# SiLU as one ScalarE function, the second part of the decay exponents as one full-array matmul, and a new order of all queues in a decoder layer

## The reference

```
xn = rmsnorm(x);  proj = xn @ w_in.T          # value, gate, B and C of 16 heads, dt
val = silu(causal_conv4(val) + conv_b)
ld = -softplus(dt + dt_bias) * exp(A_log);  cum = cumsum(ld)
M  = (C @ B.T) * where(tril, exp(cum_l - cum_m), 0)
Y  = M @ v + D_skip * v
out = (Y * silu(gate)) @ w_out.T ; out += 0.5 * memory_read(out) @ w_read.T
x  = layernorm(2 x + out)
x  = layernorm(x + layernorm(attention(x, ctx, mask)))
h  = silu(conv3(quant(x) @ quant(w1).T) + b)  # 512 hidden channels
x  = layernorm(x + quant(h) @ quant(w2).T)
```

## Time and profile before

| what | value |
|---|---|
| median of 3 runs | 895.32 us (894.7 to 895.62) |
| profiled execution, time | 894.32 us |
| profiled execution, span | 892.2 us |
| busy PE / DVE / ACT / POOL | 803.7 / 779.4 / 695.7 / 194.9 us |
| share of the span | 90% / 87% / 78% / 22% |
| granted TensorE clock, mean | 0.953 |
| ended-last chain by engine | PE 51%, DVE 26%, ACT 10%, issue 6% |

### The profile page before, as it was taken

The page is one execution under the profiler, slowest core; times in us unless marked ns, Lnnn a source line. Parts: engine busy times, 40 slices in busy tenths (PEclk is TensorE's granted clock), DMA queues, the critical chain, the costliest instruction groups (busy, mean ns, idle before and its releaser), DMA issues.

```text
span 892.2 us, 21288 instructions
## 1 busy us (share of the span) xinstructions
PE 803.7 (90%) x7928; PEld 589.3 (66%) x7928; DVE 779.4 (87%) x2286; ACT 695.7 (78%) x1372; POOL 194.9 (22%) x237
## 2 busy tenths in 40 slices
PE   3899999999999999999999999999999999966431
PEld 3667677777777677777777776777777777634221
DVE  4565679999999999999999999999999999897755
ACT  2786788888889898898888898988888888754432
POOL 6300013121220313131212202131313121223121
PEclk9899999999999999999999999999999999998555
DMA  6311110211020211110210202011111101000000
GB/s 188 74 18 25 25 37 14 49 33 17 26 48 26 46 28 37 38 37 14 57 16 30 44 25 47 27 38 36 37 25 47 17 28 34 21 18 12 0 12 24
DMA packets 51586, 30.64 MB, mean 34 GB/s; under 512 B 40442, under 2 KB 42444, under 8 KB 51484
## 3 DMA queue, kind: packets, MB, share of 16 engines
q1 hardware_dynamic: 51052, 28.17, 13.8%
q10 hardware_dynamic: 432, 1.11, 0.4%
HBM read 16.68 MB, written 4.19 MB: 23 GB/s over the span
## 4 chain that ended last, share of the span: by engine, by line
PE 51%; DVE 26%; ACT 10%; issue 6%; SPq 2%; POOL 1%; DMA 1%; ACTq 0%; POOLq 0%; DVEq 0%
PE pM L2384 6%; PE pP L2334 5%; PE pP L2336 4%; PE pP L2335 4%; DVE fa L1778 3%; DVE hm L1795 3%; PE pDec L2371 3%; DVE fa L1780 2%; PE pDec L2368 2%; DVE u L1786 2%; ACT L771 2%; DVE ML L1658 2%; DVE conv L1604 2%; PE pC L2507 2%; PE pC L2478 2%
## 5 line engine op out<-in xcount | busy, mean ns | idle before, releaser
L2334 PE MATMUL pP<-xn_hi,G_hi 128*128 128x256 f32 x512 | 157.9, 308 | 1.0 <-ACT P L746 1.0
L746 ACT ACTIVATE P<-pP 128x512 f32<-128x512 f32 x256 | 148.1, 598 | 11.6 <-PE pP L2336 10.5
L2335 PE MATMUL pP<-xn_lo,G_hi 128*128 128x256 f32 x512 | 144.0, 281 | 0.0
L2336 PE MATMUL pP<-xn_hi,G_lo 128*128 128x256 f32 x512 | 143.8, 281 | 0.0
L2384 PE MATMUL pM<-P,xnT 128*64 128x512 f32 x512 | 133.7, 597 | 0.3
L2334 PEld LDWEIGHTS pP<-xn_hi,G_hi 128*128 128x128 f32 x512 | 97.3, 190 | 18.0 <-issue 10.3
L2335 PEld LDWEIGHTS pP<-xn_lo,G_hi 128*128 128x128 f32 x512 | 97.7, 191 | 3.2 <-issue 0.7
L1658 DVE TENSOR_TENSOR ML<-pM,Lm 128x512 f32<-128x512 f32 x128 | 87.6, 684 | 14.0 <-PE pM L2384 11.6
L2336 PEld LDWEIGHTS pP<-xn_hi,G_lo 128*128 128x128 f32 x512 | 97.2, 190 | 0.0
L604 POOL TENSOR_TENSOR rs_c<-ve_c,half_pow 128x4 f32<-128x4 f32 x48 | 48.5, 1011 | 197.8 <-DVE nm_c L1750 100.9
L595 POOL TENSOR_TENSOR u<-u,fa 128x512 f32<-128x512 f32 x32 | 40.8, 1276 | 226.3 <-ACT u L846 226.3
(11 more groups left out here) (240 smaller groups left out, 2055.2 us busy)
## 6 DMA issues: line engine op xcount, KB each, us to landing
v_nat<-vT SPq DMA_DIRECT2D x256, 32.0 KB, 2.1
x_in<-in_x SPq DMA_DIRECT2D x16, 256.0 KB, 2.8
x_res<-in_x SPq DMA_DIRECT2D x16, 256.0 KB, 2.6
ctxT<-in_ctx_t SPq DMA_DIRECT2D x16, 256.0 KB, 3.0
out_x<-x SPq DMA_DIRECT2D x16, 256.0 KB, 2.0
P<-in_wc ACTq DMA_DIRECT2D x2, 512.0 KB, 6.6
P<-in_wb SPq DMA_DIRECT2D x2, 512.0 KB, 9.0
fa<-in_w_t SPq DMA_DIRECT2D x1, 256.0 KB
```

The costliest lines, as they stand in the source:

```text
L746: act.activation(P[:, half, 2 * pair:2 * pair + 2, 0:w], pP[k % 2][:, 0:2 * w].rearrange("p (h l) -> p h l", h=2), ACT.Copy).then_inc(p_co ...
L2334: pe.matmul(dst, w_hi, x_hi, start=True, stop=False)
L2335: pe.matmul(dst, w_hi, x_lo, start=False, stop=False)
L2336: return pe.matmul(dst, w_lo, x_hi, start=False, stop=True)
```

## The change

1. SiLU is one ACT instruction (`ACT.Silu`) for values, gates and all four feed-forward blocks. The products on DVE (values, gates, c = 2, 3) and on POOL (c = 0, 1) go, with their semaphores; so do the factors of 2, and the two set-up instructions for them. The gate part is now freed for pA by ACT itself.
2. conv gets two slots, fa four. `hidden_abs` writes into fa, and the buffer ha goes. The normalised input is written in place (xs is x_in), so the next load of x waits for PE's transposes.
3. A second copy of cum, cum2, holds two column blocks per unit, one for each head of a pair. POOL writes it (`spread_cum`, two instructions per group) from cum3 after `place_cum`, and `decay` of a group's first unit waits for it. The second part of the exponents is then one matmul with 128 array columns.
4. All queues (fill, body, drain) have a new order.

```
-            def value_silu(n, jj):
-                dve.wait_ge(val_tanh.sem, val_tanh.at(n, jj + 1))
-                v = vT[n % 2][:, jj, 0:width(n)]
-                dve.scalar_tensor_tensor(v, v, 1.0, flat(conv[:, 0:seqs_in(n), :]),
-                                         ALU.add, ALU.mult).then_inc(vT_ready.sem, 1)
...
-            def value_tanh(n, jj):
+            def value_silu(n, jj):
                 act.wait_ge(a_read.sem, a_read.at(n, A_VAL[jj]))
                 act.wait_ge(v_nat_ready.sem, v_nat_ready.at(n - 2, 16 * V_MOVES))
                 act.wait_ge(yd_ready.sem, yd_ready.at(n - 2, 2))
-                act.activation(vT[n % 2][:, jj, 0:width(n)], flat(conv[:, 0:seqs_in(n), :]), ACT.Tanh, scale=0.5)\
-                   .then_inc(val_tanh.sem, 1)
+                act.activation(vT[n % 2][:, jj, 0:width(n)], flat(conv[:, jj, 0:seqs_in(n), :]), ACT.Silu)\
+                   .then_inc(vT_ready.sem, 1)
...
-            def gate_tanh_step(n, jj):
+            def gate_silu(n, jj):
                 act.wait_ge(a_mm.sem, a_mm.at(n, A_GATE[jj]))
                 act.wait_ge(Yg_ready.sem, Yg_ready.at(n - 2, 2))
-                act.activation(gT[n % 2][:, jj, 0:width(n)], pA[:, 0:width(n)], ACT.Tanh, scale=0.5).then_inc(gate_tanh.sem, 1)
+                act.activation(gT[n % 2][:, jj, 0:width(n)], pA[:, 0:width(n)], ACT.Silu).then_inc(a_read.sem, 1)
...
-            def ffn_tanh(d, c):
+            def ffn_silu(d, c):
                 act.wait_ge(d_read.sem, d_read.at(d, D_H + c))
-                act.activation(u[:, c, 0:late_width(d)], flat(fa[:, c % 2, 0:late_seqs(d), :]), ACT.Tanh, scale=0.5)\
-                   .then_inc(f_tanh.sem, 1)
+                act.activation(u[:, c, 0:late_width(d)], flat(fa[:, c, 0:late_seqs(d), :]), ACT.Silu)\
+                   .then_inc(u_ready.sem, 1)
...
+            def spread_cum(n):
+
+                pool.wait_ge(a_read.sem, a_read.at(n, A_CT))
+                pool.wait_ge(dec_mm.sem, dec_mm.at(n - 2, UNITS))
+                for h2 in range(2):
+                    last = pool.tensor_scalar(cum2[n % 2][0:CUM_ROWS, 0:seqs_in(n), h2, :], cum3[n % 2][0:CUM_ROWS, 0:seqs_in(n), :],
+                                              sel[:, HH + h2:HH + h2 + 1], None, ALU.mult)
+                last.then_inc(cum_spread.sem, 1)
...
-                for h2 in range(2):
-                    last = pe.matmul(pDec[64 * h2:64 * h2 + 64, :], cum3[g % 2][:, s, :], negR[:, h2, :],
-                                     start=False, stop=True)
-                last.then_inc(dec_mm.sem, per_unit(g))
+                pe.matmul(pDec[:, :], flat(cum2[g % 2][:, s, :, :]), negR[:, :], start=False, stop=True)\
+                    .then_inc(dec_mm.sem, per_unit(g))
...
-                gate_tanh_step(0, 1)
+                gate_silu(0, 1)
```

More of the change, by code:

```diff
@@ L243, in build @@
         P = sb("P", [128, 2, H, HALF * L])
+        cum2 = [sb(f"cum2_{i}", [128, GS, 2, L], BF16) for i in range(2)]
         own_head = sb("own_head", [128, HH, 128], BF16)
-        negR = sb("negR", [128, 2, HH * L], BF16)
+        negR = sb("negR", [128, HH * L], BF16)
         sel = sb("sel", [CUM_ROWS, HH + 2])
@@ new lines, in body @@
+                cum_transposed(g)
+                maxima_transposed(g - 3)
+                decay(g - 1, 6)
+                head_pair(g, 0, 5)
+                weights_transposed(g - 2)
+                scores(g - 1, 6)
+                attend(g - 2)
+                v_transposed(g, 0)
+                head_pair(g, 0, 6)
+                scales_spread(g - 3)
+                decay(g - 1, 7)
+                keys(g - 1)
+                v_transposed(g, 1)
+                scores(g - 1, 7)
+                head_pair(g, 0, 7)
@@ L2903, in drain @@
                 head_pair(12, 0, 3)
-                x1_transposed(10)
-                decay(11, 6)
-                scores(11, 5)
                 queries(10)
@@ new lines, in drain @@
+                head_pair(13, 0, 5)
+                maxima_transposed(10)
+                decay(12, 6)
+                weights_transposed(11)
+                scores(12, 6)
+                attend(11)
+                v_transposed(13, 0)
+                decay(12, 7)
+                scales_spread(10)
+                head_pair(13, 0, 6)
+                v_transposed(13, 1)
+                decay(13, 0)
+                scores(12, 7)
+                keys(12)
+                x_transposed(14)
@@ new lines, in drain @@
+                maxima_transposed(11)
+                decay(13, 6)
+                weights_transposed(12)
+                scores(13, 6)
+                attend(12)
+                scales_spread(11)
+                v_transposed(14, 0)
+                decay(13, 7)
+                head_pair(14, 0, 6)
+                head_pair(14, 0, 7)
+                v_transposed(14, 1)
+                keys(13)
+                scores(13, 7)
+                head_pair(14, 1, 0)
+                x_transposed(15)
@@ L3218, in _ @@
             drain()
-        for chain in (ch_z, ch_a, ch_c, ch_d, ch_l, ch_u, ch_o, ch_exp, ch_b, ch_e):
+        for chain in (ch_z, ch_a, ch_c, ch_d, ch_l, ch_o, ch_exp, ch_b, ch_e):
             assert chain.k == chain.per
```

2011 lines of the change are left out of this document (938 added, 1073 removed).

## The result

| | before | after |
|---|---|---|
| median (4 runs each, same chip) | 895.07 us | 905.07 us |
| ratio, with its 95% interval | | 1.0114 [1.0085, 1.0143] |
| profiled span | 892.2 us | 901.9 us |
| granted TensorE clock, mean | 0.953 | 0.945 |

The account below looks back on a forecast made before the run. DVE, busy 47.3 of 48.9 us per period, was taken as the bound. Twelve periods 1.5 us shorter give 18 us and the end 2: 894.3 - 18 - 2 = 874.3, plus 1.0 for the median, so 875, range 856 to 896.

Parts of the forecast that it names:

- DVE is the bound: Steady period: DVE, busy 47.3 of 48.9 us, has least room; products leaving it free 65.8 us, 4.1 per group.
- Order and sum: Whole program: twelve periods 1.5 us shorter give 18 us, the end 2 us, the fill 0.
- A period of 47.4: Steady groups: ACT's 45.4 us plus 2.0 for idle time and the v_nat wait.
- the rival of another loop: Steady period: PE with hidden waits is already at its floor, so only the end gains; 892 to 895, chance 0.12.
- v_nat, PE waits 1.6 us: Steady groups: sixteen issues in line land v_nat 12.9 us behind the first SiLU; PE waits 1.6 us.
- The rival "values arrive late": Mid-period: PE waits for v_nat, the loop grows to 51.0 us, time 918; chance 0.13.
- Second part of the exponents, 0: PE: one full-array matmul for two side-by-side halves gains 0; the range's other end was 1.6 us per group.
- spread_cum, hidden: POOL's cum2 copies before a group's first exponents, 3.1 us, cost nothing under PE's other work.
- Table loads, SiLU: ACT: two more loads per group, 1.283 us each, 2.57 in all, no idle time beside them; SiLU 635 ns like tanh.
- the rival in which a load empties ACT: ACT: each new load costs its length again, period 50.0 us, time 906; chance 0.03.
- The fill, 0 ± 4, and the end: Fill: 0, up to 4 us either way; end: 2 us gained, between 6 gained and 4 lost.
- The terms priced at 0 for the second slots and for x in place: For x in place: the next load waits for PE's transposes, issued half a period or more before its statistics; 0.

Follow-up runs that it names:

- experiment 4: The kernel before without its 96 products on DVE and 64 instructions on POOL, tanh left, order kept: 879.76 us, ratio 0.9835.
- experiment 3: The changed kernel with ACT's first value SiLU right behind the first hidden SiLU and SyncE's move_v ahead of load_c: 893.92 us, ratio 1.0004.
- experiment 9: The run of experiment 3 with Tanh in place of Silu in three places, 36 table loads fewer: 884.65 us, ratio 0.9892.
- experiments 7, 8: Full-array exponents and POOL's spreading copies added to the kernel before (905.82 us, ratio 1.0132), then to the run of experiment 4 (890.93 us, ratio 0.9962).
- experiment 12: The run of experiment 3 with v_transposed of groups 0 to 2 later in PE's queue, place_v moved along on ACT: 889.11 us, ratio 0.9939.
- experiment 5: The run of experiment 4 with SiLU for tanh in the old order, factors 0.25 and 0.5 taken out of the weights: 1016.56 us, ratio 1.1358.
- experiment 2: The changed kernel with the second part of the exponents as two half-array matmuls again: 924.27 us, ratio 1.0325.
- experiment 1: The changed kernel with Tanh in place of Silu in three places, all 36 new table loads gone: 901.33 us, ratio 1.0081.
- experiments 5 and 6: The second of these: the run of experiment 5 with ACT's SiLUs drawn together, 98 table loads instead of 150: 984.50 us, ratio 1.1004.

## Why the prediction was wrong

*DVE is the bound.* Right in so far as experiment 4 gained 14 us without the products. The busy total fell by 53 us and not by the 65.8 of the earlier trace rows, because those rows overlap their neighbours (each took 0.55 us of the engine, close to the 0.52 to 0.68 of the chain in the earlier trace rows).

*Order and sum.* This is the step that failed. The sum took a period of 47.4 us, found for the steady groups alone, over twelve periods, and put the fill at 0, with the values' chain of DMA issues priced only where ACT's other rows cover it. The parts of it, beside the table of stretches:

| stretch | forecast | measured | off by |
|---|---|---|---|
| fill | 0 | +9.0 | 9.0 |
| groups 4 to 12 | -12 (47.4 each) | -1.1 (48.81 each) | 10.9 |
| groups 12 to 15 | -4.5 | +7.3 (51.4 each) | 11.8 |
| group 15 to the end | -3.5 | -5.5 | -2.0 |

Together 30 us, which is the distance from 875 to 905. The runs take it apart so, by the spans of their profiled executions. The order of two queues, undone in experiment 3, is 11.5 of it: 1.6, 5.8 and 7.4 in the first three stretches, less 3.3 in the last. The new loads on top of that, experiment 9, are 7.7: 2.5, 3.3, 0.6 and 1.4. Some 10.6 are left: 4.9 in the fill, 1.8 in groups 4 to 12 and 3.9 in groups 12 to 15. What causes these was not taken apart. With values first and no added loads, the span is still 5.0 us above that of experiment 4 (882.7 and 877.7), and its fill 7.3 above (190.3 and 183.0).

*A period of 47.4.* Too short by 1.4 us: 0.7 is the late values (48.81 to 48.08 on average), 0.4 the loads (to 47.67). That leaves 0.2. So the best period of the runs is close to the sum's, but no run with the loads in it came under 48.0 on average. PE's figure, "not to be taken at its word", was a warning all the same: with its products gone the old order stops at 47.94, only 1.0 below 48.95. That is the rival of another loop, which I gave 0.12 and priced at no gain; the truth lay between.

*v_nat, PE waits 1.6 us.* The chain was seen (sixteen issues, 0.64 us apart) and its length was right: 12.9 us were said, and from the end of the first SiLU to PE are 13.3. The wait was 0.4 to 1.1 us in steady groups, less than I said. But the sum left out two things. The new order puts load_c with its wait for m_rows ahead of move_v, so the issues start with the mask where the mask is later than the value: 0.7 us in a steady group, 12.2 us in group 12. The rule to name what is queued behind a waiting instruction would have found it. And the chain was priced in the body only, while in the fill it costs 15.8 us of PE's waiting (without any mask in the way) and at groups 12 and 13 6.3. The rival "values arrive late" had the mechanism, but not its size or place: its period of 51.0 compares with 48.81 measured, and its chain started at a product of vT instead of the mask.

*Second part of the exponents, 0.* The two halves do run side by side, as the earlier trace rows showed, but the row behind the pair was a matmul on a part of the array. The change of mode behind the pair did not show in it. The end of the range (1.6 us a group, if anything) was nearer the right size in the new order: 19 us over 16 groups is 1.2.

*spread_cum, hidden.* Right in the new order as far as the waits of the changed kernel show, wrong in the old one (experiments 7, 8). The cover I named, the work between the sums and the first exponents, is what the new order brings in the steady groups; in the fill the copies come to light once the values are not late (experiment 12).

*Table loads, SiLU.* 1283 ns, no idle time ahead, SiLU 637 ns against tanh's 635: all as the rows of before said. ACT came to 741.6 as forecast. By the Trainium skill's page "ScalarE: Activation LUTs", section "What ACT_TABLE_LOAD costs", a switch would cost 2.66 us, 1.38 of it a drain; but for the first load of the program, which stands at its start, no gap of that size shows at a load of the changed kernel. What the new loads cost the whole kernel is 4 to 9 us, where the sum had 2.6 in the end and nothing elsewhere. The measured 905 is also the number of the rival in which a load empties ACT (906), by luck: its mechanism, idle time at each load, is not there.

*The fill, 0 ± 4, and the end.* The fill lost 9.0, far outside my bounds, since a new order of several hundred steps was costed there by its loads alone. The last stretch gained 5.5, of which the sum had 3.5. The terms priced at 0 for the second slots and for x in place were in every run of the new order and stand untested.

## What to carry to other kernels

Price a DMA chain from what starts it: the instruction ahead of it in the issuing queue and that instruction's wait, not the tile that it moves. Price it once per stage, since a fill or the last groups have none of the cover of a steady period. A busy share near the whole period is no floor: look whether the chain of a steady period stays on that engine. And an edit's worth belongs to its order: the full-array matmul gave 19 us where full-array work follows, and together with its copies it cost 11 where half-array work follows; SiLU's loads cost 4 to 9 us where all of a group's stand in one run, while SiLU scattered over the old order cost 137 us (experiment 5 against 4).

## What the runs showed of the hardware

- Going from full-array to half-array matmuls costs 0.08 us at the start and 0.13 behind (0.33 against 0.25 and 0.34 against 0.21 us between starts, experiment 2), with the columns unchanged.
- A table load is 1283 ns in every row of every run, 35 to 150 of them, with some 0.02 us of idle time ahead of one on average (but for the first of the program). What one costs the kernel ran from 0.1 us (experiment 1, in which the gain is hardly clear of the noise) to its full length where it stands on the chain (experiment 5).
- SyncE's issues are 0.64 us apart with nothing else in their way, so sixteen small transfers hold its queue for 10 us, longer than the 2.9 us from the last one's issue to its landing.
- PE waiting for work was granted a lower clock: 0.94 in the steady periods of experiments 5 and 6 and 0.88 from 40 to 90 us of the changed kernel, against 1.00 in the stretches of experiment 4 and of the earlier trace rows that answer to them. In experiment 5 it was 0.50 from 403 to 407 us, behind a wait of 5.6 us that ended at 401. 1.00 is 2.4 GHz and 0.50 is 1.2; the values between are means over time at both.
